# v's tiles moved in front of the hf tile, and one probability tile copied by VectorE

## The chip, the cores and the metric

One core of one Trainium2 chip runs the whole kernel. The metric is the device time of one execution in microseconds (us). Engines are named as in the profile: PE (TensorE matmul), PEld (TensorE weight load), DVE (VectorE), ACT (ScalarE), POOL (GpSimd), SP (SyncE, which issues the DMAs).

## The reference

128 graphs of 64 nodes with 256 features go through two layers, each followed by a residual and a LayerNorm. The first is attention with 8 heads of 32 under eight masks (six fixed ones, the last two from `adj`). The second is a graph layer with 4 heads, whose masked scores go through tanh instead of softmax.

```python
# layer 1 (8 heads), then x = layernorm(x + .)
q, k, v = split_heads(x @ Wq.T + bq), split_heads(x @ Wk.T + bk), split_heads(x @ Wv.T + bv)
scores = jnp.where(mask, einsum('bhsd,bhtd->bhst', q, k) * SCALE, -1e9)
out = einsum('bhst,bhtd->bhsd', softmax(scores), v) ... @ Wo.T + bo
# layer 2 (4 heads), then x = layernorm(x + .)
Wh = einsum('bni,hoi->bhno', h, W) + bW
e = einsum('bhno,hop->bhnp', Wh, attn)
scores = einsum('bhnp,bhmp->bhnm', e, Wh)
A_mat = tanh(where(adj, scores, 0))
hp = relu(einsum('bhnm,bhmo->bhno', A_mat, Wh))
ha, hf = cat(hp) @ A_w.T, h @ fc_w.T
coeff = sigmoid(hf @ g1_w.T + ha @ g2_w.T + gbias)
return hf * coeff + ha * (1 - coeff)
```

## The kernel before

**Tiling.** The 128 graphs go in 16 groups of 8 graphs, 512 tokens each. A software pipeline works on two groups at once: a turn, `turn(A, B, more)`, does the attention layer of group A and the graph layer of the group before it, B = A - 1 (`turn(i, i - 1, True)`). `whole` calls turn 0 (set-up, group 0 alone), turn 1, turns 2 to 14 in a hardware loop, turn 15, and a last turn with a graph layer and no attention. So fifteen turns have both layers; the edits touch these.

**Precision.** Most products are made of three: every operand is split into a high part (type fp32r) and a low part (the rest), and hi x lo, lo x hi and hi x hi are added up in PSUM. ACT writes the high part when it empties a PSUM bank (`..._hi`), and DVE then reads the same bank again, subtracts the high part and writes the low part (`..._lo`); with that DVE gives the bank back. Four products are plain fp32 on PE: the attention scores (L489), the graph scores `adj` (L575), the transposes (L502, L545, L645) and attention times v (L520).

**Order and banks.** All engines run a program written out by hand. PE's accumulators are the eight PSUM banks; each tile of a turn has a fixed bank, in the order of the text `BODY` (L48): `T3:7` is tile T3 in bank 7. PE waits with `claim` until the tile before in that bank has been given back (`take`, semaphore `taken`), and the readers wait for `full`. In one turn PE makes, in this order: eight tiles T of G x hT (L380, L381, L385) with the attention scores after the first; the tile hf0 (the same three lines, 6 matmuls); the graph scores adj0 and adj1 (L575, 32 matmuls in array tiles of 128x64, `adj_scores`); v0 and v1 (L372 to L374, 24 matmuls, `values`); four transposes of the probabilities probT0 to probT3 (L502, 16 matmuls, `probs_T`); eight tiles U (L598, 48 matmuls in array tiles of 64x128, `gathered`); attention (L520, 128 matmuls in array tiles of 64x32); hf1; then cat, y, ha, z, hT, q, k and R.

**What the readers do for this stretch.** For each half of adj, ACT applies tanh (L815, into `Abuf`), DVE multiplies with the adjacency (L1039), ACT makes the high part (L819, `A_hi`), and DVE the low part (L1043, `A_lo`), which U waits for (`A_ready`, one count for each half; the first four tiles of U need half 0, the last four half 1). ACT then copies v0 and v1 (L779), the four PT tiles (L788) and U's high parts (L834); DVE makes U's low parts (L936). Attention waits for banks 7 and 4, which U's first two tiles U000 and U001 held, so for DVE's first two low parts; it also waits for all PT and v copies.

Of the kernel before, what the change touches and what calls it, by code (L numbers as in the profile page):

```python
# [16 lines left out]
H2 = 4  # L17
NG = 8
NP = NG // 2
# [18 lines left out]
def listed(text):  # L38
# [6 lines left out]
FIRST = listed("Q0:0 Q1:1 K0:2 K1:3 score0:0 score1:1 score2:2 score3:3 M0:4 M1:5 M2:6 M3:7 M4:4 M5:5 M6:6 M7:7 v0:0 "  # L45
               "probT0:1 probT1:2 G0:4 G1:5 G2:6 G3:7 probT2:3 probT3:0 v1:1 G4:4 G5:5 G6:6 attn0:2 attn1:3 "
               "W0:7 W1:4 W2:5 W3:6 y0:0 y1:1 G7:7 q0:2 q1:3 FC:4 FF:5 hT0:0 hT1:1 k0:2 k1:3")
BODY = ("T0:4 score0:0 score1:1 score2:2 score3:3 T1:5 T2:6 T3:7 T4:4 T5:5 T6:6 T7:7 hf0:4 adj0:5 adj1:6 v0:0 v1:1 "  # L48
        "probT0:2 probT1:3 probT2:0 probT3:1 U000:7 U001:4 U010:5 U011:6 U100:2 U101:3 U110:0 U111:1 attn0:7 attn1:4 "
        "hf1:5 cat0:6 cat1:2 cat2:3 cat3:7 y0:0 y1:1 cat4:4 cat5:5 cat6:6 cat7:7 ha0:4 ha1:5 z0:6 z1:7 hT0:2 hT1:3 ")  # L50
TURN = listed(BODY + "q0:0 q1:1 k0:2 k1:3 R0:6 R1:7")
# [7 lines left out]
def stage_kernel(nc, x, xT, adjS, adjT, masks, eye, wq, bq, wk, bk, wv, bv, wo, bo,  # L59
                 Wn, attn, AwT, fcn, g1T, g2T, gb, out):  # L60
    ctx = ExitStack()
    with ctx:
# [178 lines left out]
        def await_tile(eng, which, name, g):  # L241
            b, count = place_of(which, name, g)
            eng.wait_ge(full[b], count + 1)
            return BANK[b]

        def take(ins, which, name, g):
            ins.then_inc(taken[place_of(which, name, g)[0]], 1)
# [122 lines left out]
        def _(pe):  # L370
# [186 lines left out]
            def h_fc(g, c):  # L557
                if c == 0 and not later(g):
                    pe.wait_ge(ff_ready, 1)
                bank = claim(pe, "B", f"hf{c}", g)  # L560
                filled(dense(bank[:], [
                    (FF, (hT_hi, hT_lo), lambda t, k=k: t[:, k, c * P:c * P + P], lambda t, k=k: even_first(t[:, k, :]))
                    for k in range(DC)]), "B", f"hf{c}", g)
# [75 lines left out]
            def res_T(g):  # L639
                pe.wait_ge(resT_ready, g * DC + DC)  # L640
                for q2 in range(2):
                    bank = claim(pe, "B", f"R{q2}", g)
                    for q in range(2):
                        for c in range(DC):
                            ins = pe.transpose(bank[:, q * D + c * P:q * D + c * P + P],  # L645
                                               tile_cols(rT[:, c, :], 2 * q2 + q), ident[:])
                    filled(ins, "B", f"R{q2}", g)

            def turn(A, B, more):
                if B is None:  # L650
                    warm_up()
                    queries(0)
                    keys(0)
                    scores(0)
                    M1_products(range(H2 * DC))
                    values(0, 0)
                    probs_T(0, range(2))
                    G_products(range(4))
                    probs_T(0, range(2, JB))
                    values(0, 1)  # L660
                    G_products(range(4, 5))
                    attention(0, range(1))
                    G_products(range(5, 7))
                    attention(0, range(1, DC))
                    W_transposed()
                    project(0)
                    G_products(range(7, H2 * DC))
                    queries(1)
                    gate_weights()
                    h_T(0)  # L670
                    keys(1)
                    return
                for n in range(KC):
                    T_tile(B, n)
                    if A is not None and n == 0:
                        scores(A)
                    if A is None and n == 1:
                        res_T(B - 1)
                h_fc(B, 0)
                adj_scores(B)  # L680
                if A is None:
                    h_fc(B, 1)
                    gathered(B)
                    gate_h(B)
                    heads_out(B, range(KC))
                    h_a(B)
                    gate_a(B)
                    res_T(B)
                    return
                values(A, 0)  # L690
                values(A, 1)
                probs_T(A, range(JB))
                gathered(B)
                attention(A, range(DC))
                h_fc(B, 1)
                heads_out(B, range(KC // 2))
                project(A)
                heads_out(B, range(KC // 2, KC))
                h_a(B)
                gate_h(B)  # L700
                h_T(A)
                gate_a(B)
                if more:
                    queries(A + 1)
                    keys(A + 1)
                    res_T(B)
# [4 lines left out]
        def _(act):  # L711
# [96 lines left out]
                bank = await_tile(act, "B", f"hf{c}", g)  # L808
                take(act.activation(hf[:, c, :], bank[:], ACT.Copy), "B", f"hf{c}", g)

            def adj_tanh(g):
                for q2 in range(2):
                    part = slice(2 * q2, 2 * q2 + 2)
                    bank = await_tile(act, "B", f"adj{q2}", g)
                    ins = act.activation(Abuf[:, part, :, :], bank[:].rearrange("p (q h n) -> p q h n", q=2, h=H2),  # L815
                                         ACT.Tanh)
                    take(ins, "B", f"adj{q2}", g)
                    act.wait_ge(A_masked, g * 2 + (q2 + 1))
                    act.activation(A_hi[:, part, :, :], Abuf[:, part, :, :], ACT.Copy).then_inc(A_hi_ready, 1)  # L819

            def h_high(g):
                act.wait_ge(h_ready, g * NP + NP)
# [38 lines left out]
            def turn(A, B, more):  # L861
                if B is None:
                    early()
                    queries(0)
                    value_weight()
                    masks_in()
                    keys(0)
                    M1_copies(range(1))
                    exps(0, 0)
                    M1_copies(range(1, 3))  # L870
                    exps(0, 1)
                    M1_copies(range(3, 6))
                    out_weight()
                    exps(0, 2)
                    M1_copies(range(6, H2 * DC))
                    values(0, 0)
                    exps(0, 3)
                    late()
                    probs_T(0, range(2))
                    G_high(range(4))  # L880
                    probs_T(0, range(2, JB))
                    values(0, 1)
                    G_high(range(4, 5))
                    x_split(1, x_second)
                    G_high(range(5, 7))
                    attention(0)
                    W_high()
                    G_high(range(7, H2 * DC))
                    queries(1)
                    fc_high()  # L890
                    h_T(0)
                    h_high(0)
                    gate_high()
                    keys(1)
                    return
                for n in range(KC):
                    T_out(B, n)
                    if A is None and n == 1:
                        res_out(B - 1)
                    if A is not None and n in EXP_AFTER:  # L900
                        exps(A, EXP_AFTER.index(n))
                h_fc(B, 0)
                adj_tanh(B)
                if A is None:
                    h_fc(B, 1)
                    U_high(B, range(2))
                    cat_high(B, range(KC))
                    h_a(B)
                    gate(B)
                    res_out(B)  # L910
                    return
                values(A, 0)
                values(A, 1)
                probs_T(A, range(JB))
                U_high(B, range(2))
                attention(A)
                h_fc(B, 1)
                cat_high(B, range(KC // 2))
                if more:
                    x_split(A + 1)  # L920
                cat_high(B, range(KC // 2, KC))
                h_high(A)
                h_a(B)
                h_T(A)
                gate(B)
                if more:
                    queries(A + 1)
                    keys(A + 1)
                    res_out(B)
# [4 lines left out]
        def _(dve):  # L934
# [99 lines left out]
            def masked(g):  # L1034
                dve.wait_ge(adjT_in, g * 16 + 16)
                for q2 in range(2):
# [6 lines left out]
                    dve.tensor_tensor(A_lo[:, part, :, :], Abuf[:, part, :, :], A_hi[:, part, :, :].bitcast(F32),  # L1043
                                      ALU.subtract).then_inc(A_ready, 1)

            def U_low(g):
                for n, (q2, c, b) in enumerate(U_TILES):
                    first = b * D + q2 * P
                    hi, lo = (t[:, c, :, first:first + P] for t in (U_hi, U_lo))
                    dve.wait_ge(U_hi_ready, g * len(U_TILES) + (n + 1))  # L1050
                    take(low(lo, bank_of("B", f"U{q2}{c}{b}", g)[:].rearrange("p (h t) -> p h t", h=H2), hi),
                         "B", f"U{q2}{c}{b}", g)
# [77 lines left out]
            def turn(A, B, more):  # L1130
# [28 lines left out]
                if A is not None:  # L1159
                    shift(A, 1)  # L1160
                    softmax_rest(A)
                masked(B)
                U_low(B)
                if A is None:
                    cat_low(B, range(KC))
# [174 lines left out]
```

## Time and profile before

| | |
|---|---|
| median of 3 runs | 1116.5 us (1112.35 to 1117.24) |
| the profiled execution, its own time | 1114.91 us |
| its span, first to last instruction | 1113.1 us |
| outside the span | 1.8 us |
| one turn of the loop | 66.27 us |
| PE, DVE, ACT, POOL busy, share of the span | 98%, 64%, 49%, 25% |

The profile is of one execution. Starts are microseconds from the first instruction. PE's rows overlap: a matmul's row lasts longer than the distance to the next row, because the engine is pipelined, so distances between starts are the measure of what a matmul costs. The rows of ACT and DVE overlap by some 0.1 us in the same way.

### The profile page before, as it was taken

How to read it: one execution, taken by the hardware profiler on the slowest of the kernel's cores; microseconds unless marked ns; L12 is line 12 of the kernel's file. 1: busy time of each engine (PE TensorE's matmuls, PEld its weight loads, DVE VectorE, ACT ScalarE, POOL GpSimd, SP SyncE). 2: the span in 40 equal slices, each digit the busy share in tenths (PEclk: the TensorE clock that was granted, in tenths of full speed). 3: DMA queues.
4: the chain of work that ended last, by engine and by line, in shares of the span. 5: the costliest groups of instructions: out<-in, count | busy, mean ns of one | idle time of the engine just before them, and what ended most of it. 6: DMA issues, size and time to landing. Idle time of an engine off the chain costs nothing.

```text
span 1113.1 us, 25068 instructions
## 1 busy us (share of the span) xinstructions
PE 1090.0 (98%) x10018; PEld 911.4 (82%) x10018; DVE 711.7 (64%) x1353; ACT 542.1 (49%) x958; POOL 281.3 (25%) x247
## 2 busy tenths in 40 slices
PE   7999999999999999999999999999999999999995
PEld 5878888888888888888888888888788888888774
DVE  6666765757666666765757666575765666676543
ACT  3654463635536364563735546363563635445351
POOL 1533222232312313222232312213221231322200
PEclk8999999999999999999999999999999999999998
DMA  7000100001010000100001010000100100010000
GB/s 258 2 22 22 40 23 21 19 21 39 21 38 22 20 19 21 39 21 20 22 20 37 21 39 21 20 19 21 39 21 20 40 20 19 21 40 3 1 19 19
DMA packets 26699, 32.58 MB, mean 29 GB/s; under 512 B 4400, under 2 KB 23344, under 8 KB 26288
## 3 DMA queue, kind: packets, MB, share of 16 engines
q1 hardware_dynamic: 26672, 32.19, 8.6%
q8 instruction: 20, 0.33, 0.1%
q14 instruction: 7, 0.06, 0.0%
HBM read 23.80 MB, written 8.39 MB: 29 GB/s over the span
## 4 chain that ended last, share of the span: by engine, by line
PE 96%; DVE 1%; DMA 1%; ACT 1%; issue 0%; SPq 0%; POOL 0%; POOLq 0%; DVEq 0%
PE bank L380 17%; PE bank L381 17%; PE bank L385 17%; PE bank L372 8%; PE bank L374 8%; PE bank L373 8%; PE bank L575 5%; PE bank L598 4%; PE bank L489 3%; PE bank L502 3%; PE bank L520 2%; PE bank L645 1%; PE bank L545 1%; PE bank L408 1%; DMA bias_v<-in_bv 1%; PE bank L420 1%
## 5 line engine op out<-in xcount | busy, mean ns | idle before, releaser
L840 ACT ACTIVATE cat_hi<-bank 128x512 fp32r<-128x512 f32 x128 | 76.6, 598 | 127.0 <-PE bank L385 127.0
L805 ACT ACTIVATE T<-bank 128x512 f32<-128x512 f32 x128 | 76.6, 599 | 102.6 <-PE bank L385 100.8
L936 DVE SCALAR_TENSOR_TENSOR cat_lo<-bank,cat_hi 128x512 fp32r<-128x512 f32 x128 | 86.5, 686 | 38.9 <-ACT cat_hi L840 36.8
L936 DVE SCALAR_TENSOR_TENSOR U_lo<-bank,U_hi 128x512 fp32r<-128x512 f32 x128 | 78.0, 682 | 50.5 <-ACT U_hi L834 50.5
L380 PE MATMUL bank<-hT_hi,g_lo 128*128 128x512 f32 x256 | 102.9, 402 | 0.0
L381 PE MATMUL bank<-hT_hi,g_hi 128*128 128x512 f32 x256 | 99.9, 390 | 0.0
L381 PE MATMUL bank<-U_hi,wt_hi 128*128 128x512 f32 x256 | 99.8, 390 | 0.0
L380 PE MATMUL bank<-U_hi,wt_lo 128*128 128x512 f32 x256 | 99.8, 390 | 0.0
L372 PE MATMUL bank<-cat_lo,aw_hi 128*128 128x512 f32 x256 | 99.6, 389 | 0.0
L373 PE MATMUL bank<-cat_hi,aw_lo 128*128 128x512 f32 x256 | 99.6, 389 | 0.0
L374 PE MATMUL bank<-cat_hi,aw_hi 128*128 128x512 f32 x256 | 99.6, 389 | 0.0
L1233 POOL TENSOR_TENSOR probs<-probs,den 128x512 f32<-128x512 f32 x64 | 66.5, 1049 | 129.6 <-DVE den L1024 129.6
L936 DVE SCALAR_TENSOR_TENSOR haT_lo<-bank,haT_hi 128x512 fp32r<-128x512 f32 x32 | 22.1, 691 | 114.4 <-ACT haT_hi L845 114.4
L1226 POOL TENSOR_TENSOR y<-y,bo_all 128x1024 f32<-128x1024 f32 x16 | 38.5, 2408 | 190.3 <-ACT at_hi L795 190.3
L845 ACT ACTIVATE haT_hi<-bank 128x512 fp32r<-128x512 f32 x32 | 19.1, 598 | 135.5 <-PE bank L374 135.5
L385 PE MATMUL bank<-U_lo,wt_hi 128*128 128x512 f32 x256 | 78.9, 389 | 0.0
L385 PE MATMUL bank<-hT_lo,g_hi 128*128 128x512 f32 x256 | 78.8, 389 | 0.0
L1216 POOL TENSOR_TENSOR hT<-hT_hi,hT_lo 128x1024 f32<-128x1024 f32 x16 | 38.3, 2395 | 108.5 <-DVE hT_lo L936 108.5
L834 ACT ACTIVATE U_hi<-bank 128x512 fp32r<-128x512 f32 x128 | 64.4, 628 | 1.4
L575 PE MATMUL bank<-T,hT 128*64 128x256 f32 x512 | 58.8, 382 | 0.0
L1113 DVE SCALAR_TENSOR_TENSOR hf<-th,hf 128x512 f32<-128x512 f32 x32 | 52.4, 1637 | 9.4 <-ACT th L850 9.4
L385 PEld LDWEIGHTS bank<-hT_lo,g_hi 128*128 128x128 f32 x256 | 48.1, 188 | 10.4
(154 smaller groups left out, 2743.3 us busy)
## 6 DMA issues: line engine op xcount, KB each, us to landing
y<-in_x SPq DMA_DIRECT2D x16, 512.0 KB, 3.6
out<-res SPq DMA_DIRECT2D x16, 512.0 KB, 3.0
x_raw<-in_xT SPq DMA_DIRECT2D x15, 512.0 KB, 3.3
W_nat<-in_Wn SPq DMA_DIRECT2D x1, 1028.0 KB, 6.1
attn_nat<-in_attn SPq DMA_DIRECT2D x1, 1024.0 KB, 8.6
adjS_u<-in_adjS SPq DMA_DIRECT2D x32, 32.0 KB, 2.7
raw_A<-in_AwT SPq DMA_DIRECT2D x1, 1024.0 KB, 8.0
x_second<-in_xT SPq DMA_DIRECT2D x1, 512.0 KB, 9.6
```

Source lines behind the costliest of these rows:

```text
L372: pe.matmul(out, asel(a[0]), bsel(b[1]), start=first, stop=False)
L373: pe.matmul(out, asel(a[1]), bsel(b[0]), start=False, stop=False)
L374: return pe.matmul(out, asel(a[0]), bsel(b[0]), start=False, stop=last)
L380: pe.matmul(out, wsel(w[1]), dsel(d[0]), start=first and n == 0, stop=False)
L381: pe.matmul(out, wsel(w[0]), dsel(d[0]), start=False, stop=False)
L385: ins = pe.matmul(out, wsel(w[0]), dsel(d[1]), start=False, stop=last and n == len(terms) - 1)
L575: ins = pe.matmul(bank[b * S:b * S + S, q * D:q * D + D].rearrange("p (h n) -> p h n", h=H2), hT[:, k, first:first + S], T[:, k, :, first: ...
L805: take(act.activation(T[:, n % DC, n // DC, :], bank[:], ACT.Copy), "B", f"T{n}", g)
L834: act.activation(U_hi[:, c, :, first:first + P], bank[:].rearrange("p (h t) -> p h t", h=H2), ACT.Copy).then_inc(U_hi_ready, 1)
L840: act.activation(cat_hi[:, n, :], bank[:], ACT.Relu).then_inc(cat_hi_ready, 1)
L936: return dve.scalar_tensor_tensor(out=out, in0=bank, scalar=bias, in1=hi.bitcast(F32), op0=op, op1=ALU.subtract)
L1233: pool.tensor_tensor(view, view, den[:, j, :].unsqueeze(2).to_broadcast([P, NG, S]), ALU.mult) \
```

## The change

On PE the two v tiles go in front of hf0, so that adj is followed directly by the transposes, U and attention; the text `BODY` is changed likewise, and the banks stay the same. On ACT the copies of v go in front of that of hf0, the tanh and the high part of each half become two functions, and the copy of PT0 stands between the tanh and the high part of half 1; PT1 and PT3 follow. PT2 is copied by DVE, behind its four operations on the graph scores. Turn 0 and the last turn keep their work and their order.

```diff
-BODY = ("T0:4 score0:0 score1:1 score2:2 score3:3 T1:5 T2:6 T3:7 T4:4 T5:5 T6:6 T7:7 hf0:4 adj0:5 adj1:6 v0:0 v1:1 "
+BODY = ("T0:4 score0:0 score1:1 score2:2 score3:3 T1:5 T2:6 T3:7 T4:4 T5:5 T6:6 T7:7 v0:0 v1:1 hf0:4 adj0:5 adj1:6 "
...
@@ tensor, turn
+                if A is not None:
+                    values(A, 0)
+                    values(A, 1)
                 h_fc(B, 0)
                 adj_scores(B)
...
-                values(A, 0)
-                values(A, 1)
                 probs_T(A, range(JB))
                 gathered(B)
                 attention(A, range(DC))
@@ scalar
-            def adj_tanh(g):
-                for q2 in range(2):
-                    part = slice(2 * q2, 2 * q2 + 2)
-                    bank = await_tile(act, "B", f"adj{q2}", g)
-                    ins = act.activation(Abuf[:, part, :, :], bank[:].rearrange("p (q h n) -> p q h n", q=2, h=H2),
-                                         ACT.Tanh)
-                    take(ins, "B", f"adj{q2}", g)
-                    act.wait_ge(A_masked, g * 2 + (q2 + 1))
-                    act.activation(A_hi[:, part, :, :], Abuf[:, part, :, :], ACT.Copy).then_inc(A_hi_ready, 1)
+            def adj_tanh(g, q2):
+                bank = await_tile(act, "B", f"adj{q2}", g)
+                take(act.activation(Abuf[:, 2 * q2:2 * q2 + 2, :, :],
+                                    bank[:].rearrange("p (q h n) -> p q h n", q=2, h=H2), ACT.Tanh), "B", f"adj{q2}", g)
+
+            def adj_high(g, q2):
+                part = slice(2 * q2, 2 * q2 + 2)
+                act.wait_ge(A_masked, g * 2 + (q2 + 1))
+                act.activation(A_hi[:, part, :, :], Abuf[:, part, :, :], ACT.Copy).then_inc(A_hi_ready, 1)
@@ scalar, turn
+                if A is not None:
+                    values(A, 0)
+                    values(A, 1)
                 h_fc(B, 0)
-                adj_tanh(B)
+                adj_tanh(B, 0)
+                adj_high(B, 0)
+                adj_tanh(B, 1)
+                if A is not None:
+                    probs_T(A, range(1))
+                adj_high(B, 1)
...
-                values(A, 0)
-                values(A, 1)
-                probs_T(A, range(JB))
+                probs_T(A, (1, 3))
                 U_high(B, range(2))
                 attention(A)
@@ vector
+            def probs_T(g, j):
+                bank = await_tile(dve, "A", f"probT{j}", g)
+                take(dve.tensor_copy(PT[:, j, :, :], bank[:].rearrange("p (q s) -> p q s", q=NP)), "A", f"probT{j}", g)
@@ vector, turn
                 masked(B)
+                if A is not None:
+                    probs_T(A, 2)
                 U_low(B)
```

PE around the graph scores, in the order of the program before (`ff` is hf0, `T,hT` the graph scores, `wv` the first of 24 matmuls of v):

```order
L381 MATMUL bank<-hT_hi,ff_hi 128x512
L380 MATMUL bank<-hT_hi,ff_lo 128x512
L381 MATMUL bank<-hT_hi,ff_hi 128x512
L385 MATMUL bank<-hT_lo,ff_hi 128x512 x2
L575 MATMUL bank<-T,hT 64x256 x16
L372 MATMUL bank<-wv_lo,x_hi 128x256
L373 MATMUL bank<-wv_hi,x_lo 128x256
L374 MATMUL bank<-wv_hi,x_hi 128x256
```

And the same place after:

```order
L374 MATMUL bank<-wv_hi,x_hi 128x256
L380 MATMUL bank<-hT_hi,ff_lo 128x512
L381 MATMUL bank<-hT_hi,ff_hi 128x512
L380 MATMUL bank<-hT_hi,ff_lo 128x512
L381 MATMUL bank<-hT_hi,ff_hi 128x512
L385 MATMUL bank<-hT_lo,ff_hi 128x512 x2
L575 MATMUL bank<-T,hT 64x256 x16
L502 MATMUL bank<-ident,probs 128x128 x16
L598 MATMUL bank<-A_hi,h_lo 128x4x64 x2
```

The 24 matmuls of v now stand ahead of hf0, and the transposes follow the graph scores without anything between.

ACT from the copy of hf0 to U's high parts, before:

```order
L809 ACTIVATE hf<-bank 128x512
L815 ACTIVATE Abuf<-bank 128x512
L819 ACTIVATE A_hi<-Abuf 128x512
L815 ACTIVATE Abuf<-bank 128x512
L819 ACTIVATE A_hi<-Abuf 128x512
L779 ACTIVATE v<-bank 128x512 x2
L788 ACTIVATE PT<-bank 128x512 x4
L834 ACTIVATE U_hi<-bank 128x4x128 x8
```

And after:

```order
L780 ACTIVATE v<-bank 128x512 x2
L810 ACTIVATE hf<-bank 128x512
L814 ACTIVATE Abuf<-bank 128x512
L820 ACTIVATE A_hi<-Abuf 128x512
L814 ACTIVATE Abuf<-bank 128x512
L789 ACTIVATE PT<-bank 128x512
L820 ACTIVATE A_hi<-Abuf 128x512
L789 ACTIVATE PT<-bank 128x512 x2
L835 ACTIVATE U_hi<-bank 128x4x128 x8
```

Between the second high part of the graph scores and U's first tile ACT had six copies, two of v and four of PT; now it has two of PT.

## Rows read from the trace of the kernel before

**Rows 1.** The page: busy us, share of the span, instructions.
```profile
PE 1090.0 (98%) x10018; PEld 911.4 (82%) x10018; DVE 711.7 (64%) x1353; ACT 542.1 (49%) x958; POOL 281.3 (25%) x247
```

**Rows 2.** Waits of PE over the whole span: us in total, times, longest.
```profile
PE bank L489 <- ACT kT L775: 4.4, 1, 4.4
```

**Rows 3.** Timeline, attention in the first and last full turn: start, us, what.
```profile
85.37 1.47 PE L520 MATMUL bank<-PT,v 64*32 64x64 f32 x128
1013.77 1.48 PE L520 MATMUL bank<-PT,v 64*32 64x64 f32 x128
```

**Rows 4.** Timeline of PE in one turn of the loop.
```profile
404.31 0.39 PE L380 MATMUL bank<-hT_hi,ff_lo 128*128 128x512 f32 x1
...
405.76 3.67 PE L575 MATMUL bank<-T,hT 128*64 128x256 f32 x32
409.37 0.39 PE L372 MATMUL bank<-wv_lo,x_hi 128*128 128x256 f32 x1
409.59 0.28 PE L373 MATMUL bank<-wv_hi,x_lo 128*128 128x256 f32 x1
...
412.34 1.91 PE L502 MATMUL bank<-ident,probs 128*128 128x128 f32 x16
414.18 0.39 PE L598 MATMUL bank<-A_hi,h_lo 64*128 64x256 f32 x2
...
417.03 0.28 PE L598 MATMUL bank<-A_hi,h_hi 64*128 64x256 f32 x2
417.26 1.48 PE L520 MATMUL bank<-PT,v 64*32 64x64 f32 x128
...
421.08 0.62 PE L385 MATMUL bank<-U_lo,wt_hi 128*128 128x512 f32 x2
```

**Rows 5.** Timeline of the weight loads in the same turn.
```profile
409.37 0.19 PEld L372 LDWEIGHTS bank<-wv_lo,x_hi 128*128 128x128 f32 x1 [0.39 <-issue]
...
415.59 0.19 PEld L598 LDWEIGHTS bank<-A_hi,h_lo 64*128 64x128 f32 x2
...
417.24 1.33 PEld L520 LDWEIGHTS bank<-PT,v 64*32 64x32 f32 x128
```

**Rows 6.** Timeline of ACT in the same turn; in brackets idle before, and releaser.
```profile
407.76 0.60 ACT L815 ACTIVATE Abuf<-bank 128x512 f32<-128x512 f32 x1 [1.28 <-PE bank L575]
409.11 0.63 ACT L819 ACTIVATE A_hi<-Abuf 128x512 fp32r<-128x512 f32 x1 [0.76 <-DVE Abuf L1039]
409.65 0.58 ACT L815 ACTIVATE Abuf<-bank 128x512 f32<-128x512 f32 x1
411.10 0.63 ACT L819 ACTIVATE A_hi<-Abuf 128x512 fp32r<-128x512 f32 x1 [0.87 <-DVE Abuf L1039]
411.64 0.58 ACT L779 ACTIVATE v<-bank 128x512 f32<-128x512 f32 x1
...
413.03 2.06 ACT L788 ACTIVATE PT<-bank 128x512 f32<-128x512 f32 x4
415.19 4.03 ACT L834 ACTIVATE U_hi<-bank 128x512 fp32r<-128x512 f32 x8
```

**Rows 7.** Timeline of DVE in the same turn.
```profile
410.38 0.68 DVE L1039 TENSOR_TENSOR Abuf<-Abuf,adjT_u 128x512 f32<-128x512 f32 x1
411.76 0.69 DVE L1043 TENSOR_TENSOR A_lo<-Abuf,A_hi 128x512 fp32r<-128x512 f32 x1 [0.70 <-ACT A_hi L819]
415.82 4.88 DVE L936 SCALAR_TENSOR_TENSOR U_lo<-bank,U_hi 128x512 fp32r<-128x512 f32 x8 [3.36 <-ACT U_hi L834]
```

**Rows 8.** Timeline, last turn: DVE's last row and the weight load it releases.
```profile
1051.08 0.69 DVE L1116 SCALAR_TENSOR_TENSOR rT<-hf,rT 128x512 f32<-128x512 f32 x1
1051.82 0.85 PEld L645 LDWEIGHTS bank<-ident,rT 128*128 128x128 f32 x8 [1.69 <-DVE rT L1116]
```

**Rows 9.** Groups of DVE by line and shape: busy us, mean ns; the nearest to a copy.
```profile
L1011 DVE TENSOR_TENSOR probs<-bank,mask_static 128x512 f32<-128x512 f32 x48 | 31.8, 663 | 4.5 <-PE bank L489 4.5
L1082 DVE TENSOR_TENSOR y<-bank,y 128x512 f32<-128x512 f32 x32 | 22.1, 691 | 13.3 <-PE bank L374 11.9
```

## The prediction

> **What bounds the kernel now.** I read the page first. PE is busy 98% of the span, and the next engine, DVE, 64% [rows 1]. A busy share alone could hide slack, since matmuls overlap, so the second view is the list of PE's waits: its longest is 4.4 us, it comes once and belongs to the set-up [rows 2]. In the timeline the fifteen attention blocks of the full turns lie 928.40 us apart from the first (85.37) to the last (1013.77) [rows 3], 66.3 us a turn, and within a turn PE goes from one block to the next without a gap worth the name [rows 4]. So PE's row of matmuls is the bound, and nothing that shortens ACT's or DVE's work shortens the run. The change adds and removes no matmul. It can move the time in two ways only: through what PE loses between two blocks, and through a wait that PE does not have now. I therefore need ACT's and DVE's timelines of one turn against PE's, to see how much earlier than needed each input is there [rows 5 to 7]. I take the turn from 404 us on, which is one of the thirteen of the loop.
>
> **v in front of hf0.** From v's second matmul (409.59) to the first transpose (412.34) are 2.75 us for 23 matmuls, 0.120 each, so 24 take 2.87 [rows 4]. hf0 started at 404.31 and the graph scores at 405.76 [rows 4]; behind v the scores start at 405.76 + 2.87 = 408.63. The transposes keep their place, 412.34, if going from scores to transposes costs what going from scores to v cost, and U keeps 414.18. v needs banks 0 and 1, which the attention scores left long before, and its copies are now two free slots of ACT ahead of hf0, where ACT waits for PE anyway (1.28 us idle before tanh) [rows 6]. That part costs nothing. What was moved closer together is the end of the graph scores and U: 2.87 us of cover for the chain tanh, mask, high part, low part are gone.
>
> **The chain behind the scores.** Every link is a distance between starts. Half 0's tanh starts 2.00 behind the scores (407.76 - 405.76), half 1's 1.89 behind that (409.65 - 407.76), because ACT does half 0's high part first [rows 4, 6]. Half 1's scores end at 3.67, so they are in time for 3.89 [rows 4]. From tanh to mask are 0.73 (409.65 to 410.38), from mask to high part 0.72 (to 411.10), from high part to low part 0.66 (to 411.76) [rows 6, 7]. After the change: tanh of half 0 at 410.63, of half 1 at 412.52, its mask at 413.25, its high part at 413.97, its low part at 414.63, done 0.69 later at 415.32. A release from DVE reaches PE's weight load 0.05 later (1051.08 + 0.69 = 1051.77, load at 1051.82) [rows 8], so 415.37. PE loads the first weights of U's second half at 415.59 [rows 5]: 0.22 to spare. Half 0, by the same links, is done 0.73 + 0.72 + 0.66 + 0.69 = 2.80 behind its tanh, at 413.43, for a need at 414.18 [rows 4]. So U itself does not wait.
>
> **PT0 between tanh and high part.** PT0's transposes are the first quarter of a block that begins at 412.34 [rows 4], full before 413.0. ACT is free from about 413.03 (0.5 behind tanh) to 413.97, when the mask is done. One copy is 2.06 us for four [rows 6], a step of 0.49 and a row of 0.58, so PT0 fits into time in which ACT would wait, and delays nothing.
>
> **PT1, PT3 and U's high parts.** Here is the price. High part to the next copy is 0.54 (411.10 to 411.64), and two PT copies are 2 x 0.49 [rows 6]: PT1 at 414.51, PT3 at 415.00, U's first high part at 415.49. Before, it started at 415.19 [rows 6], right when PE had filled the first tile of U. It comes 0.30 later. U's first low part starts 0.63 behind it (415.19 to 415.82), and eight low parts in 4.88 are a step of 0.60 [rows 7]. The second one ends at 415.49 + 0.63 + 0.60 + 0.68 = 417.40 and frees bank 4 for attention; with 0.05 for the release PE can load at 417.45. Before the change the same sum gave 417.15, and PE loaded at 417.24 [rows 5], 0.09 later than it could: PE itself was the later one. So attention starts 0.30 - 0.09 = **0.21 us later**. It can't be cheaper by an earlier end of U, since attention waits for DVE and DVE for ACT. Behind attention the shift does not grow: all eight low parts are done at 416.12 + 4.88 = 421.00, and PE needs them at 421.08 + 0.21 [rows 4].
>
> **PT2 on DVE.** It stands between the last low part of the scores and U's first. The profile has no DVE copy; its nearest rows read the same 128x512 from a bank in 663 to 691 ns [rows 9]. I take 0.69: it starts one step of DVE (0.6, as above) behind 414.63, at 415.24, and ends at 415.93, where DVE is first wanted at 416.12. Hidden with 0.2 to spare; at half that cost nothing changes, at twice that cost U's low parts start 0.5 later. Bank 0, which PT2 frees, is wanted for U's seventh tile, the last quarter of a block that starts at 414.18 and ends at 417.15, so at 416.4 [rows 4]; it is free at 415.98.
>
> **Going from one block to the next.** v's first matmul behind the scores takes 0.22 where the others take 0.12, and its weight load sat idle for 0.39 [rows 4, 5], so the step from array tiles of 128x64 to full tiles costs PE between 0.1 and 0.39. The change does not remove it; transposes in full tiles now stand there in place of v. It may be cheaper for them, by 0 to 0.39 a turn. But in the sum above it is worth nothing, since attention's start hangs on ACT. I take 0.
>
> The Trainium skill, TensorEngine Tiling (Array Packing), Key Properties, says that changing the tiling mode, not just the tile, drains TensorE. By that rule the gain is exactly nothing, for the block has five such changes before and five after; by the rows alone up to 0.39 a turn remain open, if ACT were not late.
>
> **Other queues.** SP's load of the next adjacency waits for the low parts of the scores and is issued 3 us later, for a use a turn (66 us) away. POOL's work has no part in it. Turn 0 and the last turn keep their order.
>
> **Sum.** Fifteen turns by 0.21 are 3.2 us. On the profiled execution's 1114.9 that gives 1118.1; the median of the runs shown is 1116.5, 1.6 above that execution, and gives 1119.7. I take the middle, **1119 us**, 0.3% above before. The lower end of the term is 0, if the links overlap by another 0.2; the upper end uses ACT's full row times, 0.63 + 0.60 + 0.60 instead of 0.54 + 0.49 + 0.49, which makes 0.21 + 0.31 = 0.52 a turn, 7.8 us.
>
> **The rivals.**
> 1. *Full cover, no wait.* ACT gains one PT copy and the chain is a little shorter than summed, so U's high parts start when PE has filled them. For it: only 0.2 us are between wait and no wait. Against it: each link is measured and repeats in every turn. It gives 0 to -0.1 a turn, 1114 to 1117 us.
> 2. *Cheaper step between blocks.* The scores followed by transposes lose less than the scores followed by v, and ACT is not late: up to 0.39 x 15 = 5.9 us, 1109 to 1113 us. It needs two things at once, and the second contradicts the rows.
> 3. *The second half of the scores comes late* (the slower side). Its place is the wait for `A_ready` ahead of U's fifth tile, 0.22 us from deciding. If PT0's copy ends after the mask (ACT at 413.97), by the bank being full 0.4 later than I think or the copy being longer, the high part, both PT copies and everything behind move by as much. With 0.3 more at the high part and 0.3 of rows not overlapping, attention starts 0.8 later: 12 us, 1127 us.
> 4. *The DVE copy is dear.* Twice 0.69 puts U's low parts 0.5 later than summed, 0.7 a turn, 10.5 us, 1126 us.
>
> **Chances.** The forecast 0.62, full cover 0.20, cheaper step 0.05, late second half 0.08, dear copy 0.05. A measurement of this kernel can tell about 0.5% from no change, 5.6 us or 0.37 a turn. The forecast lies within that for most of its range; I give 0.05 of it to slower, and of the cheaper step 0.04 to faster. So faster 0.04, same 0.78, slower 0.18. For 8 times in 10 the range takes in full cover with its spread over runs, 1113.5, and the forecast's upper end, 1116.5 + 7.8, less its thinnest part: 1123.5.
>
> **What would show it.** In the profile after: the scores start 2.87 behind where hf0 started; U's first high part follows PT3 without idle time and about 0.3 later relative to U's first matmul than before (1.01 now, 1.3 after); DVE's idle time before U's low parts shrinks to 0.2 and names ACT; attention's first weight load is about 0.2 later behind U's last matmul (0.21 now, 0.42 after); a turn lasts 66.5 us. It would be wrong if U's matmuls have a gap in the middle (rival 3), if DVE is not idle ahead of U's low parts (rival 4), or if attention follows U at the old distance (rivals 1 and 2).

## The result, and the profile after

The changed kernel takes 1119.85 us (median of 20 runs), the kernel before 1115.59 us (20 runs): a ratio of 1.0039, with a 95% interval of 1.0031 to 1.0046. That is 4.3 us slower, less than half a per cent, but well clear of the spread between runs. The forecast was 3.2 us slower, 1119 us, with a range of 1113.5 to 1123.5. The profiled execution took 1119.48 us, with a span of 1117.4 us.

The page of the changed kernel, busy us and share of the span, against [rows 1]:

```profile
PE 1089.3 (97%) x10018; PEld 910.3 (81%) x10018; DVE 720.5 (64%) x1368; ACT 535.8 (48%) x943; POOL 281.4 (25%) x247
```

PE does the same 10018 matmuls in the same busy time. DVE has 15 instructions more and ACT 15 fewer: the PT2 copies of the fifteen full turns. The 4 us are time in which PE waits, and the list of PE's waits (us in total, times, longest) has a line that was not there before [rows 2]:

```profile
PE bank L489 <- ACT kT L776: 4.9, 1, 4.9
PE bank L520 <- DVE U_lo L943: 4.3, 15, 0.4
```

Fifteen times attention waits for a low part of U, 4.3 us together. The timeline of PE and its weight loads in one turn of the loop, to be laid beside [rows 4, 5]; v starts at 339.55:

```profile
339.55 0.28 PE L372 MATMUL bank<-wv_lo,x_hi 128*128 128x256 f32 x1
...
343.90 3.67 PE L575 MATMUL bank<-T,hT 128*64 128x256 f32 x32
347.51 1.97 PE L502 MATMUL bank<-ident,probs 128*128 128x128 f32 x16
349.40 0.39 PE L598 MATMUL bank<-A_hi,h_lo 64*128 64x256 f32 x2
...
352.26 0.28 PE L598 MATMUL bank<-A_hi,h_hi 64*128 64x256 f32 x2
352.80 1.47 PE L520 MATMUL bank<-PT,v 64*32 64x64 f32 x128 [0.26 <-DVE U_lo L943]
```
```profile
352.77 1.34 PEld L520 LDWEIGHTS bank<-PT,v 64*32 64x32 f32 x128 [0.43 <-issue]
```

U runs without a gap from 349.40 to 352.26. Only behind its last matmul is there 0.51 us to attention's weight load, where before there were 0.21. ACT and DVE in the same turn, beside [rows 6, 7]:

```profile
347.79 0.58 ACT L814 ACTIVATE Abuf<-bank 128x512 f32<-128x512 f32 x1
348.27 0.59 ACT L789 ACTIVATE PT<-bank 128x512 f32<-128x512 f32 x1
349.24 0.63 ACT L820 ACTIVATE A_hi<-Abuf 128x512 fp32r<-128x512 f32 x1 [0.38 <-DVE Abuf L1046]
349.78 1.07 ACT L789 ACTIVATE PT<-bank 128x512 f32<-128x512 f32 x2
350.74 4.02 ACT L835 ACTIVATE U_hi<-bank 128x512 fp32r<-128x512 f32 x8
```
```profile
349.91 0.69 DVE L1050 TENSOR_TENSOR A_lo<-Abuf,A_hi 128x512 fp32r<-128x512 f32 x1 [0.70 <-ACT A_hi L820]
350.51 0.69 DVE L1055 COPY PT<-bank 128x512 f32<-128x512 f32 x1
351.37 4.88 DVE L943 SCALAR_TENSOR_TENSOR U_lo<-bank,U_hi 128x512 fp32r<-128x512 f32 x8 [0.17 <-ACT U_hi L835]
```

This is the predicted picture. PT0 lies in a hole of ACT: ACT still waits 0.38 us for the mask behind it. From the second high part on, ACT works without a pause (high part, PT1, PT3, U), so U's first high part starts 1.34 us behind U's first matmul (before: 1.01). DVE's PT2 copy ends in time, since DVE then waits another 0.17 us for ACT. A turn lasts 66.57 us, from this attention at 286.23 to 352.80; before it was 66.27.

```profile
286.23 1.47 PE L520 MATMUL bank<-PT,v 64*32 64x64 f32 x128 [0.26 <-DVE U_lo L943]
```

### The profile page after: what moved, and what is told of

It reads as the page before. It is cut to its first block, busy times and chain, and to the rows that moved or that the text cites. A ratio compares the mean times of both kernels' runs of the same rounds, so it can differ in the third digit from the quotient of the medians.

```text
span 1117.4 us, 25081 instructions
## 1 busy us (share of the span) xinstructions
PE 1089.3 (97%) x10018; PEld 910.3 (81%) x10018; DVE 720.5 (64%) x1368; ACT 535.8 (48%) x943; POOL 281.4 (25%) x247
## 4 chain that ended last, share of the span: by engine, by line
PE 86%; DVE 5%; ACT 4%; issue 3%; DMA 1%; SPq 0%; POOL 0%; DVEq 0%; ACTq 0%; POOLq 0%
PE bank L380 17%; PE bank L381 17%; PE bank L385 17%; PE bank L372 8%; PE bank L374 8%; PE bank L373 8%; PE bank L489 3%; PE bank L575 3%; PE bank L520 2%; DVE Abuf L1046 2%; PE bank L545 1%; PE bank L645 1%; DVE U_lo L943 1%; ACT A_hi L820 1%; ACT PT L789 1%
## 5 line engine op out<-in xcount | busy, mean ns | idle before, releaser
L1046 DVE TENSOR_TENSOR Abuf<-Abuf,adjT_u 128x512 f32<-128x512 f32 x32 | 22.0, 688 | 72.3 <-ACT Abuf L814 72.3
```

## The experiments

Theory 1 is the forecast's: attention hangs on DVE's second low part of U, that on ACT's first high part of U, and that on how many copies ACT has behind the second high part of the graph scores. Theory 2: DVE's new copy costs the time. Theory 3: PE loses it at its own steps, above all from the scores to the transposes. "Turn" is the distance of two attention blocks in the loop. Every ratio is to the kernel before.

### The DVE copy alone, in the order of before

```diff
@@ scalar, turn of the kernel before
-                probs_T(A, range(JB))
+                probs_T(A, (0, 1, 3))
@@ vector, turn
                 masked(B)
+                if A is not None:
+                    probs_T(A, 2)
                 U_low(B)
```

> PE and ACT in the order of the kernel before, only PT2 is copied by DVE in front of U's low parts. Theory 1 (attention waits for DVE's second low part of U, which hangs on ACT's first high part of U): here ACT has one copy less, but U's first high part can't start before PE has filled U's first tile, so it stays about 1.0 us behind U's first matmul and the turn stays at 66.27 us; ratio to before 1.000, at most 0.05 us a turn. Theory 2 (the copy on DVE is what costs, since it stands in front of U's low parts): a turn of 66.5 to 66.6 us and a ratio of 1.003 to 1.004.

Measured: ratio 0.9991 (0.9979 to 1.0003), a turn of 66.25 us (attention at 353.38 and at 419.63). ACT and then DVE:

```profile
416.66 0.60 ACT L788 ACTIVATE PT<-bank 128x512 f32<-128x512 f32 x1 [0.17 <-PE bank L502]
417.57 4.03 ACT L834 ACTIVATE U_hi<-bank 128x512 fp32r<-128x512 f32 x8 [0.31 <-PE bank L598]
```
```profile
416.23 0.69 DVE L1048 COPY PT<-bank 128x512 f32<-128x512 f32 x1 [1.39 <-PE bank L502]
418.20 4.87 DVE L936 SCALAR_TENSOR_TENSOR U_lo<-bank,U_hi 128x512 fp32r<-128x512 f32 x8 [1.28 <-ACT U_hi L834]
```

ACT waits 0.31 us for PE to fill U's first tile, DVE 1.28 us behind its copy. One copy less helps nobody where PE is the later one, and the copy on DVE costs nothing here. Theory 2 is out for the order of before. In the new order DVE has less room, so the next run takes the copy away there.

### The new order alone, all PT copies on ACT

```diff
@@ scalar, turn of the changed kernel
-                probs_T(A, (1, 3))
+                probs_T(A, (1, 2, 3))
@@ vector, turn
                 masked(B)
-                if A is not None:
-                    probs_T(A, 2)
                 U_low(B)
```

> The changed order with all four PT copies on ACT, DVE as before. Theory 1: one more copy of 0.49 us between the second high part of the graph scores and U's first high part; U's first high part 1.83 us behind U's first matmul (1.34 in the changed kernel), attention 0.49 us later, a turn of 67.05 us, 7.3 us more than the changed kernel, a ratio of 1.010 to before. Theory 2 (the DVE copy costs): the turn goes back to 66.3. Theory 3 (PE loses the time at the step from graph scores to transposes): it stays at 66.56.

Measured: ratio 1.0093 (1.0069 to 1.0116), a turn of 67.05 us, to the hundredth as expected.

```profile
421.01 1.55 ACT L789 ACTIVATE PT<-bank 128x512 f32<-128x512 f32 x3
422.44 4.04 ACT L835 ACTIVATE U_hi<-bank 128x512 fp32r<-128x512 f32 x8
```
```profile
424.52 1.48 PE L520 MATMUL bank<-PT,v 64*32 64x64 f32 x128 [0.74 <-DVE U_lo L943]
```

A third copy behind the high part puts U's first high part 0.48 us later, and attention's wait grows by as much, from 0.26 to 0.74. So the DVE copy, far from costing anything, saved the change from costing 10 us, and theory 2 is out for the new order too.

### PT0 behind the high part

```diff
@@ scalar, turn of the changed kernel
-                if A is not None:
-                    probs_T(A, range(1))
                 adj_high(B, 1)
...
-                probs_T(A, (1, 3))
+                probs_T(A, (0, 1, 3))
```

> The changed kernel, but ACT copies PT0 behind the second high part of the graph scores, with PT1 and PT3. Theory 1: three copies again between that high part and U's first high part, as when PT2 is on ACT: one step of 0.49 us more, a turn of 67.05 us, a ratio of 1.010 to before. PT0's slot in front of the high part was free. If the order of the copies doesn't matter: 66.56.

Measured: ratio 1.0090 (1.0065 to 1.0115), a turn of 67.05 us (355.31 to 422.36). It equals the run above, though a different engine does PT2. What counts is the number of copies between the high part and U, three in both; PT0's slot ahead of the high part was free. (PT0's copy also gives back bank 2 later, which U's fifth tile needs. U's last matmul comes 0.25 us later behind its first than in the changed kernel; that lies within attention's wait and costs nothing here.)

### PT2 copied twice on DVE

```diff
@@ vector, probs_T of the changed kernel; scrap lies over kT, which is not in use then
                 bank = await_tile(dve, "A", f"probT{j}", g)
+                dve.tensor_copy(scrap[:], bank[:])
                 take(dve.tensor_copy(PT[:, j, :, :], bank[:].rearrange("p (q s) -> p q s", q=NP)), "A", f"probT{j}", g)
```

> The changed kernel, with a second copy of PT2's bank on DVE, into a buffer that nobody reads. DVE sat idle for 0.17 us ahead of U's low parts; a second copy of 0.61 uses that and pushes the low parts by 0.44. Theory 1: attention 0.44 us later, a turn of 67.0 us, 6.6 us more than the changed kernel, a ratio of 1.010 to before. If DVE's low parts do not gate attention (PE or the PT copies on ACT do), the turn stays at 66.56.

Measured: ratio 1.0078 (1.0057 to 1.0099), a turn of 66.91 us (356.87 to 423.78), 0.34 more than the changed kernel, where 0.44 were expected.

DVE, then PE inside U:

```profile
421.15 0.69 DVE L1056 COPY scrap<-bank 128x512 f32<-128x512 f32 x1
421.75 0.68 DVE L1057 COPY PT<-bank 128x512 f32<-128x512 f32 x1
422.35 4.87 DVE L944 SCALAR_TENSOR_TENSOR U_lo<-bank,U_hi 128x512 fp32r<-128x512 f32 x8
```
```profile
422.18 0.28 PE L599 MATMUL bank<-A_hi,h_hi 64*128 64x256 f32 x2
422.58 0.39 PE L599 MATMUL bank<-A_hi,h_lo 64*128 64x256 f32 x2
```

Two copies cost 1.20 between starts, and the low parts follow at once. DVE's cover was 0.26 us, not the 0.17 of its idle time: a row is 0.69 long, but the next can start 0.60 behind it. Attention moved with the low parts (its weight load is 0.12 us behind the second one's end, as in the changed kernel), so they gate it. The later copy also gives back bank 0 later: U's seventh tile starts 0.40 behind the matmuls before it, where the others are 0.12 apart. PE's last matmul of U (423.25) is still 0.50 ahead of attention's load (423.75), so that gap doesn't decide. This is rival 4's mechanism, and it is real, but the copy would have had to be 0.26 us dearer before it began.

### PT0 on DVE too

```diff
@@ scalar, turn of the changed kernel
-                    probs_T(A, range(1))
+                    probs_T(A, (1,))
                 adj_high(B, 1)
...
-                probs_T(A, (1, 3))
+                probs_T(A, (3,))
@@ vector, masked(g, A), called as masked(B, A): between mask and low part
+                    if q2 == 1 and A is not None:
+                        probs_T(A, 0)
                     dve.wait_ge(A_hi_ready, g * 2 + (q2 + 1))
                     dve.tensor_tensor(A_lo[:, part, :, :], ...
```

> The changed order, but DVE copies PT0 too, between the mask and the low part of the second half of the graph scores, and ACT copies PT1 in PT0's slot and only PT3 behind the second high part. Theory 1: U's first high part is bound by PE again, 1.0 us behind U's first matmul; DVE is free for the low parts 0.07 us later than that would allow; attention starts 3.12 us behind U's first weight load (3.37 in the changed kernel, 3.06 before), a turn of 66.29 to 66.33 us, a ratio of 1.000 to 1.001 to before. Theory 3: it stays at 66.56. If DVE's copy does not fit in front of the low part (slot of 0.77 us for a copy of 0.69), U's second half starts late and the turn is 66.4 or more.

Measured: ratio 1.0003 (0.9990 to 1.0017), a turn of 66.31 us (350.85 to 417.16), as expected. DVE and the weight load:

```profile
413.75 0.68 DVE L1057 COPY PT<-bank 128x512 f32<-128x512 f32 x1
414.53 0.69 DVE L1052 TENSOR_TENSOR A_lo<-Abuf,A_hi 128x512 fp32r<-128x512 f32 x1
415.13 0.68 DVE L1057 COPY PT<-bank 128x512 f32<-128x512 f32 x1
415.74 3.67 DVE L943 SCALAR_TENSOR_TENSOR U_lo<-bank,U_hi 128x512 fp32r<-128x512 f32 x6
```
```profile
417.13 1.34 PEld L520 LDWEIGHTS bank<-PT,v 64*32 64x32 f32 x128 [0.18 <-issue]
```

With one copy behind the high part instead of two, U's first high part is back at 1.02 us behind U's first matmul, and the change costs 0.04 us a turn, too little to show in the time. It gains nothing either. The low parts still follow DVE's own chain, so attention's load (3.11 us behind U's first) remains 0.05 later than before.

### The wait taken away: half of two low parts left out

DVE's low parts of U's first two tiles cover half the columns, which frees attention's banks earlier; the other half is set to zero, so that half is left out of the result's low part. (In the texts below, e5 and e6 are the first pair, the kernel before and the changed one; e9 and e10 are the second pair, the changed one and the kernel before.) In a first pair of runs, one of either kernel, the zeroing stood in front of DVE's last low part:

```diff
@@ vector, U_low, of either kernel
+                    hs = slice(0, 2 if n < 2 else H2)
+                    if n == len(U_TILES) - 1:
+                        for m in range(2):
+                            dve.memset(U_lo[:, 0, 2:H2, m * D:m * D + P].bitcast(F32), 0.0)
-                    hi, lo = (t[:, c, :, first:first + P] for t in (U_hi, U_lo))
+                    hi, lo = (t[:, c, hs, first:first + P] for t in (U_hi, U_lo))
...
-                    take(low(lo, bank_of(...)[:].rearrange("p (h t) -> p h t", h=H2), hi),
+                    take(low(lo, bank_of(...)[:].rearrange("p (h t) -> p h t", h=H2)[:, hs, :], hi),
```

> The kernel before, but the low parts of U's first two tiles cover half the columns (the other half is set to zero later, behind DVE's seventh low part, so part of U's low part is left out). The two banks that attention waits for are free 0.5 us earlier. Question: was attention in the kernel before already held by DVE, by about a tenth of a microsecond, or did PE come later than the bank? If held (weight load 0.13 us behind DVE's second low part, as in the changed kernel and in the three others): attention moves to less than 3.06 us behind U's first weight load, down to 2.95 if the step from U to attention costs nothing more, and the turn gets up to 0.1 us shorter, a ratio of 0.9985. If PE was the later one, as the prediction had it: 3.06 and 66.27 us stay. The zeroing delays the last low part by some 0.2 us, which PE would feel only from 0.3.

> The changed kernel with the same halved low parts of U's first two tiles. Theory 1: attention's release is 0.5 us earlier than needed to remove its wait; it starts 2.95 to 3.06 us behind U's first weight load (3.37 in the changed kernel), the turn goes to 66.2 to 66.3 us, a ratio of 1.000 to before, and the wait of PE's attention for DVE is gone. Theory 3 (time lost at PE's own steps): 66.5 or more.

Measured: the kernel before with it 1.0012 (0.9998 to 1.0026), a turn of 66.36; the changed kernel with it 1.0055 (1.0038 to 1.0072), a turn of 66.70 (352.21 to 418.91). The second missed its expectation by 0.4 us a turn, the first by 0.1. Attention's wait in the loop was gone, but each list of waits had a new one, first the kernel before, then the changed one:

```profile
PEld bank L385 <- DVE U_lo L936: 3.8, 16, 0.2
PEld bank L385 <- DVE U_lo L943: 8.3, 16, 0.5
```

The zeroing takes 0.46 us, more than I had allowed, and cat0's last two matmuls wait for the last low part of U. The edit had moved the wait and not removed it. The pair says that this second gate is close behind the first, and nothing on the question asked of it. So the zeroing was put where DVE is idle, ahead of the scores' mask:

```diff
@@ vector, turn (and hs in U_low as above)
+                for m in range(2):
+                    dve.memset(U_lo[:, 0, 2:H2, m * D:m * D + P].bitcast(F32), 0.0)
                 masked(B)
```

> The changed kernel with halved low parts of U's first two tiles as in e6, but the zeroing of the other half stands on DVE ahead of the graph scores' mask, where DVE is idle for 4 us, and not inside the chain of low parts. e6 removed attention's wait and got a new one at cat0, 0.5 us, for the last low part. Theory 1: with both gone the turn is what PE alone takes in the new order, 66.25 to 66.29 us, attention 3.06 us behind U's first weight load, a ratio of 1.000 to before, and no wait of PE or of its weight loads names U_lo. If PE's own steps in the new order cost time, 66.4 or more.

> The kernel before with the same edit as e9, as its control: no low part of U can hold PE. If PE was the later one in the loop of the kernel before, the turn stays at 66.27 us and attention at 3.06 us behind U's first weight load, and only the two full turns outside the loop get 0.1 us shorter. e9 minus e10 is then what the new order costs or gains on PE itself: 0.00 to -0.05 us a turn if the number of changes of array tile is what counts.

Measured: the changed kernel with it 1.0003 (0.9989 to 1.0016), a turn of 66.25 us; the kernel before with it 0.9995 (0.9984 to 1.0006), a turn of 66.23 us. First the changed kernel's attention, then that of before:

```profile
351.42 1.48 PE L520 MATMUL bank<-PT,v 64*32 64x64 f32 x128
...
417.67 1.48 PE L520 MATMUL bank<-PT,v 64*32 64x64 f32 x128
```
```profile
352.62 1.48 PE L520 MATMUL bank<-PT,v 64*32 64x64 f32 x128
...
418.85 1.48 PE L520 MATMUL bank<-PT,v 64*32 64x64 f32 x128
```

Neither list of waits has one of PE for U's low parts. (In the two full turns outside the loop the changed kernel still loads attention's first weights 0.23 us behind the second low part; what follows is of the loop.) The two differ by 0.02 us a turn. That is the whole of what PE's new order costs by itself, and theory 3 is out. Of the changed kernel's 66.57, 66.25 are PE's own work and 0.32 are the wait for DVE.

The kernel before lost 0.04 us, where the expectation was 66.27 unchanged. Weight loads, first of U and of attention in this run, then U's in the kernel before, where attention's is at 417.24 [rows 5]:

```profile
415.79 0.19 PEld L598 LDWEIGHTS bank<-A_hi,h_lo 64*128 64x128 f32 x2 [0.17 <-issue]
...
418.85 1.32 PEld L520 LDWEIGHTS bank<-PT,v 64*32 64x32 f32 x128
```
```profile
414.18 0.19 PEld L598 LDWEIGHTS bank<-A_hi,h_lo 64*128 64x128 f32 x2 [0.17 <-issue]
```

The load is 3.06 us behind U's first load in both, so DVE did not hold it in the kernel before. The first matmul of attention was 0.02 us behind its load there (417.26) and starts with it here (418.85). That is half of the 0.04; the other half is not placed.

### One change of array tile more

```diff
@@ the kernel before: banks in BODY
-... U111:1 attn0:7 attn1:4 hf1:5 cat0:6 ...
+... U111:1 hf1:7 attn0:4 attn1:5 cat0:6 ...
@@ tensor, turn (and the same swap on scalar)
-                attention(A, range(DC))
                 h_fc(B, 1)
+                attention(A, range(DC))
```

> The kernel before with hf1 (six matmuls in full tiles) between U and attention instead of behind attention, with the banks hf1:7, attn0:4, attn1:5. Attention then has 1.4 us more time for its banks, so no wait of any kind for DVE's low parts, but PE changes its array tiles once more in a turn (64x128 to full to 64x32 to full, instead of 64x128 to 64x32 to full). If each change costs PE what the rows of before suggest (0.1 to 0.3 us), the turn is 66.35 to 66.55 us, a ratio of 1.001 to 1.004; if the change of tiles costs nothing and only the wait for DVE mattered: 66.2 us.

Measured: ratio 1.0021 (1.0008 to 1.0034), a turn of 66.45 us (353.25 to 419.70), with no wait of PE for DVE's low parts. Weight loads:

```profile
418.12 0.19 PEld L380 LDWEIGHTS bank<-hT_hi,ff_lo 128*128 128x128 f32 x1
...
419.70 1.32 PEld L520 LDWEIGHTS bank<-PT,v 64*32 64x32 f32 x128 [0.36 <-issue]
...
421.11 0.19 PEld L380 LDWEIGHTS bank<-U_hi,wt_lo 128*128 128x128 f32 x1
```

Against the kernel before without any wait (66.23), one more change of array tile costs 0.22 us a turn. So the price that the prediction's second rival needed exists. The change in question collects none of it; it leaves the number of changes in this stretch at five. The prediction cited the Trainium skill, TensorEngine Tiling (Array Packing), Key Properties, for the rule that a change of the tiling mode drains TensorE. These runs agree in what follows from it: the same number of changes, 0.02 us; one more, 0.22. That the cost is a drain they don't show.

## Why the prediction was right, and where its size was off

**Direction and place** held: attention waits for DVE's second low part, in every full turn, and in the loop nothing on PE's row but the blocks that were moved shifted by as much as 0.1 us. The size was too small: 0.21 us a turn against a measured 0.29, 3.2 us in all against 4.3. The base of the sum, the middle of 1114.9 and 1116.5, is 1115.7 and fits the 1115.6 of twenty runs, so the 0.9 us between 1119 and 1119.85 are in the term. The range of 10 us is more than twice the effect and also held "no change"; it is the trace, not the total, that decides between the forecast and rival 1.

**v in front of hf0.** Predicted 4.32 us from v's start to the scores' (408.63 against 404.31); measured 4.35 (339.55 to 343.90). That the copies of v are free also held. (Its list of signs says that the scores start 2.87 behind where hf0 started; its own sum says 2.87 behind where the scores started, and that is what to look for.)

**The chain behind the scores.** Predicted from the scores' start to U's first high part: 6.86; measured 6.84. To the end of the second low part: predicted 8.77, measured 351.37 + 0.60 + 0.68 - 343.90 = 8.75. Distances between starts, taken link by link from the trace before, carried to a rearranged chain within 0.02 us. The rows' lengths would have given 0.3 too much.

**PT0, PT2 and the second half of the scores** were hidden as costed: 0.38 us of ACT's wait left over, 0.26 of DVE's, and no gap inside U (its first to its last matmul 349.40 to 352.26, 2.86 us; 2.85 before). Rivals 3 and 4 did not happen.

**The step from scores to transposes** was taken at 0. It is a cost of 0.02 for the order as a whole; rival 2 had nothing to collect.

**The mis-sized term is the release.** The prediction took 0.05 us from DVE's end to PE's weight load, from a row in which an idle PE waited in the last turn [rows 8], and so found that in the kernel before "PE itself was the later one", by 0.09. Here the release takes 352.77 - 352.65 = 0.12. In the kernel before, DVE's second low part ended at 417.10; with 0.12 that is 417.22, against a load at 417.24 [rows 5]. The spare was 0.02, not 0.09. In the loop PE was the later one, as the half-low run of before shows (attention's load keeps its distance of 3.06 us from U's first load), but only just. With that, 0.21 a turn becomes 0.28 and, with hf0's 0.03 less the chain's 0.02, the measured 0.29.

**The two full turns outside the loop** were counted like the others. They lose 0.45 and 0.38 us. There the release takes 0.23 to 0.24 us by the rows, in both kernels. In the last full turn before, DVE's second low part ended at 1012.22 + 0.60 + 0.68 = 1013.50 and PE loaded at 1013.74; in the changed kernel it ends at 1017.04 + 0.60 + 0.68 = 1018.32, and PE loads at 1018.55. First before, then after:

```profile
1012.22 4.88 DVE L936 SCALAR_TENSOR_TENSOR U_lo<-bank,U_hi 128x512 fp32r<-128x512 f32 x8 [3.29 <-ACT U_hi L834]
1013.74 1.34 PEld L520 LDWEIGHTS bank<-PT,v 64*32 64x32 f32 x128 [0.23 <-issue]
```
```profile
1017.04 3.08 DVE L943 SCALAR_TENSOR_TENSOR U_lo<-bank,U_hi 128x512 fp32r<-128x512 f32 x5 [0.17 <-ACT U_hi L835]
1018.55 1.34 PEld L520 LDWEIGHTS bank<-PT,v 64*32 64x32 f32 x128 [0.62 <-issue]
```

So here the kernel before had nothing to spare: attention was already held by DVE, by 0.10 us (its load comes 3.16 us behind U's first load; in the half-low run of before 3.06). "PE itself was the later one" is wrong for these two turns, and they pay the whole delay of U's first high part, 1.01 us behind U's first matmul before and 1.40 after.

**The sum** with the measured terms is 13 x 0.29 + 0.45 + 0.38 = 4.6 us. The medians differ by 4.3, with an interval of 3.5 to 5.1, and the sum lies in it. The two profiled executions differ by 4.6 (1114.91 to 1119.48), their spans by 4.3. That agreement should not be taken for more than it is: single executions differ by more than that outside the part that was changed. The attention block of the first full turn starts at 85.37 us before and at 87.53 in the run with the DVE copy alone, whose turn is no longer. The last eight matmuls of the program, for which PE has sat idle for 2.21 us in both, take 1.73 us before and 1.09 after: in the execution of before the granted clock falls from the 2.4 GHz level to that of 1.2 GHz among them (0.66 on average from 1102 to 1104 us), in the other it falls only behind them.

**What can be told apart.** The prediction put the smallest difference that a measurement can show at 0.5%. Twenty runs of each kernel gave 0.39% with an interval from 0.31 to 0.46%, so a slowdown of this size is no longer "no change".

**Rival 1** (full cover) was worth its place: 0.3 us of ACT's time decide. The run with PT0 on DVE brings U's first high part back to 1.02 us behind U's first matmul, and the turn to 66.31 us.

## What to carry to other kernels

Where the bound engine passes a point with hundredths of a microsecond to spare, taking cover from a chain costs nearly in full: here 0.32 us at U's first high part became 0.29 us a turn. Add the chain up by distances between starts, and take the release from a wait of the same kind and place, not from the nearest one at hand. When a block is moved closer to its inputs, count the instructions that other engines still have queued between the last link of that chain and the first reader: here a third copy cost 0.48 us a turn, whichever copy it was, and with one copy instead of two 0.26 of the change's 0.30 were gone. Moving matmuls together while the number of changes of array tile stays the same moved PE by 0.02 us a turn, and one change more cost 0.22; that one change fewer would give as much back was not run.

## What the hardware showed that was not expected

- The time from the end of a DVE instruction to PE's weight load that waits for it was 0.05 us in the last turn [rows 8], 0.12 at attention in the loop, and 0.23 at attention outside the loop, in both kernels. In both places the program waits through the same calls; what makes the difference was not tested.
- One change of array tile more costs PE 0.22 us a turn, with the same matmuls.
- A DVE copy of 128x512 fp32 from PSUM takes 0.69 us and lets the next instruction start after 0.60. Two zeroings of 128x256 in two strided pieces each took 0.46 us between starts; I had allowed 0.2.

```profile
416.95 0.68 DVE L1055 COPY PT<-bank 128x512 f32<-128x512 f32 x1
417.80 4.06 DVE L943 SCALAR_TENSOR_TENSOR U_lo<-bank,U_hi 128x256 fp32r<-128x256 f32 x7 [0.17 <-ACT U_hi L835]
421.86 0.55 DVE L1063 MEMSET U_lo<- 128x256 f32 x2
422.32 0.63 DVE L943 SCALAR_TENSOR_TENSOR U_lo<-bank,U_hi 128x512 fp32r<-128x512 f32 x1
```

These rows are DVE's in the changed kernel with the zeroing inside the chain: from 421.86 to 422.32 for both pieces.
